# A first norm by row factors: centred weights, a factor per pixel from DRAM, and x turned three images ahead

## The chip, the cores and the metric

The kernel runs on one core of a Trainium2 chip. The metric is the device time of one execution in microseconds. A core has TensorE (matrix products and transposes into PSUM), VectorE, ScalarE and GpSimd (element work), SyncE (here it only issues transfers, on one queue) and 16 DMA engines. Each engine works off its own list in order, and engines wait for each other through semaphores.

## The reference

The input x has 16 images of 128 channels and 32 x 32 pixels. One block of a network is computed, in float32:

```python
# _ln_c: norm over the 128 channels of each pixel, eps 1e-6
x = x + conv(_ln_c(x))
#   conv: q, k, v = w_qkv @ net (8 heads of 32); k = softmax(k) over the 1024 pixels
#         context = k v^T per head; out = context q; w_out @ out + b_out
t = tokens(x)                       # (16, 1024, 128)
# _ln_t: norm over the 128 channels of each token, eps 1e-5
t = t + ffn(_ln_t(t))
#   ffn: feat = mean over the 16 images; w = softmax(feat @ Wr + br)  (1024 x 8)
#        8 experts: relu(bn(x W1 + b1)), relu(bn(. W2 + b2)), . Wo + bo; sum weighted by w
x = channels(t)
```

The weights of the experts belong to the pixel's place, and depend on the mean over all images. So the experts can't start before all images are through the attention and the second norm.

## The kernel before, in words

**First pass, in rounds.** `rounds` (L204) runs a `step` for t = -2 to 15; one round handles image t, prepares image t+1 and t+2, and finishes t-1 to t-3. On each engine the body of `step` is the list in its order. Per image:

- SyncE loads x (channels by pixels). TensorE turns it into tokens (`turn`, L539, into `p_k`), ScalarE copies it to `xT` (L778), VectorE takes `bn_stats` (L1039) and seven small operations (`statistics`, L1051), and GpSimd the power -1/2 and the shift (L1240, L1242). So each token has a factor RSTD and a SHIFT.
- GpSimd makes xn in token layout, `xnT` (`norm`, L1244, eight pieces of 128 x 128, L1248). TensorE turns xn back to channels (`turn_xn`, L504, into `p_tok`), ScalarE rounds it to `xn_hi` (L796), VectorE takes the rest, `xn_lo` (L996). All large products are sums of three: hi x hi, lo x hi, hi x lo.
- `k_half` (L548): k = wk xn, 2 x 6 products of 512 columns. VectorE finds each row's maximum (`head_max`, L1067), ScalarE takes the exponential E (`exp_half`, L840). TensorE turns E by halves (`turn_e`, L565, four times four transposes, all into one bank `p_e`), ScalarE copies it (`move_e`, L835), and `add_g` (L576) adds up G = xn^T E over the eight chunks, for each of two halves of the latent.
- In the next round: `gT` (L751), the product by heads (`heads_out`, L478), `y` (L967), `m` (L437), its high and low part (L766, L980), `add_m` (L487: M xn into `p_chan`), and x1 = x + M xn + b (L1011), stored to DRAM. So q, v, the context and w_out are folded into one 128 x 128 matrix M per image.
- In round t+2, x1 is turned and copied (`x1T`, L760), and has its statistics; its norm is shared by ScalarE (four pieces, L809) and GpSimd (four), into `xn2T`, and added to `feat` by GpSimd in round t+3 (L1300). The two rows SHIFT and RSTD are turned by one transpose (`turn_rows`, L496), copied (`move_rows`, L822) and stored to DRAM (L311), for the expert pass, which reads them back as rows over all partitions.

Weights are prepared in between: W1 and W2 are scaled by the batch norm, W1 is shifted by the mean (`shift_weights`, L521), w_out is spread by heads (L1020) and multiplied (L428).

**Passage.** Behind the last round the engines' lists are written out: the last x1, its norms, the mean `feat`, the logits, the routing (eight transposes of the routing into PSUM, copied to `routeT`, L913), 3 x 8 transposes that spread the weights of experts 0 to 2 over the partitions, the others by broadcast from DRAM (L350), with first products of experts in between.

**Second pass.** `slots` (L268): 16 images x 8 experts, three layers of 6 products each. TensorE is the one that never waits there.

The order around the change is fixed by hand: by the lists, by one SyncE queue for all transfers, and by the semaphores.

Of the kernel before, what the change touches and what calls it, by code (L numbers as in the profile page):

```python
# [24 lines left out]
F32 = mybir.dt.float32  # L25
# [20 lines left out]
TWO_MEAN, DIFFERENCE, SQUARES, BETWEEN, MINUS_MEAN, WITHIN, VARIANCE, SHIFT, RSTD = range(9)  # L46
# [13 lines left out]
def metaformer_kernel(nc, x, w_qkv, w_out, b_out, Wr, br, W1, W2, Wo, small, bo, ident_in, heads_in, out):  # L60
# [20 lines left out]
    MIDDLE = 6  # L81
    x1_dram = nc.dram_tensor("x1_scratch", [IMAGES, C, PIXELS], F32, kind="Internal").ap()
    rows_dram = nc.dram_tensor("rows_scratch", [IMAGES, 1, 2 * PIXELS], F32, kind="Internal").ap()
    route_dram = nc.dram_tensor("route_scratch", [EXPERTS, PIXELS], F32, kind="Internal").ap()

    with ExitStack() as ctx:  # L86
# [46 lines left out]
        const = sb("const", [128, len(CONSTANTS), CHUNKS])  # L133

        x_in = [route_all[:, p] for p in (6, 7)]
        x_res = [sb(f"x_res{p}", [C, PIXELS]) for p in range(2)]
        xnT = [as_tokens(n) for n in (4, 5)]
        sb("spacer", [128, 48])
# [3 lines left out]
        ekT = [as_tokens(n) for n in (2, 3)]  # L142
# [10 lines left out]
        rows_out = [sb(f"rows_out{p}", [2 * CHUNKS, 128]) for p in range(2)]  # L153
        row_bias = sb("row_bias", [2 * CHUNKS, 1])
        rows = sb("rows", [128, 2 * PIXELS])
        st = [sb(f"st{k}", [128, CHUNKS, 6]) for k in range(2)]
        ln = [sb(f"ln{k}", [128, 9, CHUNKS]) for k in range(2)]
# [4 lines left out]
        p_late = banks(6, 2)  # L162

        ident_loaded, small_loaded = sem("ident_loaded"), sem("small_loaded")
        x0_loaded, x0_turned, x0_copied = sem("x0_loaded"), sem("x0_turned"), sem("x0_copied")
        xn0_turned, xn0_hi_done, xn0_lo_done = sem("xn0_turned"), sem("xn0_hi_done"), sem("xn0_lo_done")
# [3 lines left out]
        in_loaded = [sem(f"in_loaded{p}") for p in range(2)]  # L170
# [6 lines left out]
        wT_done, wk_hi_done, wT_moved = sem("wT_done"), sem("wk_hi_done"), sem("wT_moved")  # L177
# [6 lines left out]
        xnt_done, x1t_done, last_turned = sem("xnt_done"), sem("x1t_done"), sem("last_turned")  # L184
# [8 lines left out]
        norm1_first = sem("norm1_first")  # L193
        stats_done = [stats1_done, stats2_done]
        sums_done = [sem(f"sums_done{k}") for k in range(2)]
        terms_done = [sem(f"terms_done{k}") for k in range(2)]
        var_done = [sem(f"var_done{k}") for k in range(2)]

        rstd_done = [sem(f"rstd_done{k}") for k in range(2)]
        ln_done = [sem(f"ln_done{k}") for k in range(2)]  # L200
        norm2_middle = sem("norm2_middle")
        norm1_done, norm2_last, feat_done = sem("norm1_done"), sem("norm2_last"), sem("feat_done")

        def rounds(engine, step):  # L204
# [4 lines left out]
            for t in range(-2, 5):  # L209
                step(t, t % 2, **valid(t))  # L210
# [3 lines left out]
            for t in range(IMAGES - 3, IMAGES):  # L214
                step(t, t % 2, **valid(t))
# [1180 lines left out]
```

## Time and profile before

| | us |
|---|---|
| three runs | 793.59, 792.53, 790.49; median 792.53 |
| the profiled execution | 792.24 |
| its span (first to last instruction) | 790.4 |
| start, up to the k product of image 0 | 15.05 |
| the 16 rounds, to the last G product | 223.2 |
| passage | 43.9 |
| expert stretch | 494.66 |

All intervals come from one profiled execution. An engine that is busy for a whole stretch sets its length. A busy share over the span averages over stretches with different limits, so the stretches are looked at one by one. The last four rows of the table are cut at the k product of image 0, at the end of the last product G (238.25), and at the last wait of TensorE ahead of the experts (282.11).

### The profile page before, as it was taken

Reading aid. Unit: us, or ns where it says so; the run is one execution under the profiler, and the core shown is the slowest. Engines: PE = TensorE matmul, PEld = TensorE weight load, DVE = VectorE, ACT = ScalarE, POOL = GpSimd, SP = SyncE. Lnnn points to the kernel's source line nnn. Section 1 sums busy time; section 2 is a strip of 40 time slices with the busy share of each in tenths; the row PEclk is TensorE's granted clock in tenths of the full one; section 3 lists DMA queues with packets and bytes.
Section 4 is the critical chain, followed back from the end, with each engine's and each line's share of the span. In section 5 each row is a group of like instructions: output and inputs, shape, how many; then the busy total and the mean of one; then the engine's idle time right before and its main releaser. Section 6 shows DMA issues by size and latency. Waiting matters only on the chain.

```text
span 790.4 us, 12762 instructions
## 1 busy us (share of the span) xinstructions
PE 775.7 (98%) x4242; PEld 648.6 (82%) x4242; DVE 527.0 (67%) x980; ACT 435.6 (55%) x570; POOL 650.9 (82%) x518
## 2 busy tenths in 40 slices
PE   8999999999998989999999999999999999999998
PEld 6998889889886778888888888888888888888886
DVE  5688787878787656666566665666656666566665
ACT  3576767676765655455454554545545455454543
POOL 5669888888888578888888888888888888888874
PEclk9999999999999999999999999999999999999999
DMA  8124233242531423031130311303113031130100
GB/s 249 54 81 142 101 124 117 99 142 80 214 120 44 158 110 134 0 134 67 67 133 0 133 60 73 133 0 133 62 71 133 0 133 59 74 133 1 54 27 27
DMA packets 22767, 72.58 MB, mean 92 GB/s; under 512 B 2880, under 2 KB 7624, under 8 KB 20688
## 3 DMA queue, kind: packets, MB, share of 16 engines
q1 hardware_dynamic: 22736, 72.19, 25.5%
q8 instruction: 17, 0.28, 0.2%
q14 instruction: 14, 0.11, 0.0%
HBM read 55.24 MB, written 16.94 MB: 91 GB/s over the span
## 4 chain that ended last, share of the span: by engine, by line
PE 67%; DVE 1%; POOL 1%; ACT 1%; issue 1%; POOLq 0%; DVEq 0%; ACTq 0%
PE psum L594 64%; PE psum L545 1%; PE psum L584 0%; PE psum L602 0%; POOLq L86 0%; POOL h_lo L1278 0%; ACT h_hi L853 0%; PE psum L702 0%; PE psum L717 0%; POOL xn2T L1248 0%; POOL ln L1240 0%; DVE st L1039 0%; DVE ln L1056 0%; PE psum L573 0%; DVE x_res L1127 0%
## 5 line engine op out<-in xcount | busy, mean ns | idle before, releaser
L1081 DVE SCALAR_TENSOR_TENSOR h_lo<-psum,h_hi 128x1024 fp32r<-128x1024 f32 x128 | 156.8, 1225 | 191.1 <-ACT h_hi L853 191.1
L853 ACT ACTIVATE h_hi<-psum 128x1024 fp32r<-128x1024 f32 x128 | 131.6, 1028 | 236.0 <-PE psum L594 236.0
L1278 POOL TENSOR_TENSOR h_lo<-w_raw,h_hi 128x1024 fp32r<-128x1024 f32 x64 | 154.1, 2409 | 41.8 <-ACT h_hi L872 41.8
L594 PE MATMUL psum<-h_hi,w_hi 128*128 128x512 f32 x382 | 118.5, 391 | 2.3 <-DVE w_raw L1102 2.3
L1102 DVE SCALAR_TENSOR_TENSOR w_raw<-psum,minus_t,route_all 128x1024 f32<-128x1024 f32 x93 | 118.6, 1275 | 1.7 <-DMA route_all<-route_scratch 1.1
L594 PE MATMUL psum<-h_lo,w_hi 128*128 128x512 f32 x382 | 119.4, 394 | 0.0
L594 PE MATMUL psum<-h_hi,w_lo 128*128 128x512 f32 x382 | 118.4, 391 | 0.0
L1278 POOL TENSOR_TENSOR xn_lo<-feat_most,xn_hi 128x1024 fp32r<-128x1024 f32 x31 | 74.7, 2409 | 36.0 <-ACT xn_hi L872 36.0
L594 PEld LDWEIGHTS psum<-h_hi,w_hi 128*128 128x128 f32 x382 | 71.4, 188 | 19.7 <-issue 2.7
L594 PEld LDWEIGHTS psum<-h_lo,w_hi 128*128 128x128 f32 x382 | 71.9, 188 | 15.6
L1240 POOL TENSOR_TENSOR ln<-ln,const 128x8 f32<-128x8 f32 x32 | 52.6, 1643 | 38.5 <-DVE ln L1065 38.5
L594 PEld LDWEIGHTS psum<-h_hi,w_lo 128*128 128x128 f32 x382 | 71.8, 188 | 15.2
L594 PE MATMUL psum<-xs_lo,w_hi 128*128 128x512 f32 x252 | 78.5, 393 | 0.0
L594 PE MATMUL psum<-xs_hi,w_hi 128*128 128x512 f32 x252 | 78.1, 391 | 0.0
L594 PE MATMUL psum<-xs_hi,w_lo 128*128 128x512 f32 x252 | 78.1, 391 | 0.0
L1278 POOL TENSOR_TENSOR xn_lo<-w_raw,xn_hi 128x1024 fp32r<-128x1024 f32 x32 | 77.0, 2405 | 0.9 <-ACT xn_hi L872 0.9
L872 ACT CAST h_hi<-w_raw 128x1024 fp32r<-128x1024 f32 x64 | 66.7, 1042 | 2.2 <-DVE w_raw L1102 2.2
L584 PE MATMUL psum<-route_all 128*128 128x128 f32 x512 | 65.7, 276 | 0.0
L584 PEld LDWEIGHTS psum<-route_all 128*128 128x128 f32 x512 | 62.8, 191 | 1.3
L845 ACT ACTIVATE route_all<-psum,negmax 128x1024 f32<-128x1024 f32 x32 | 35.7, 1116 | 36.8 <-DVE negmax L1074 36.0
L594 PEld LDWEIGHTS psum<-xs_hi,w_hi 128*128 128x128 f32 x252 | 47.1, 188 | 10.7
L594 PEld LDWEIGHTS psum<-xs_lo,w_hi 128*128 128x128 f32 x252 | 47.3, 188 | 10.2
(192 smaller groups left out, 1489.7 us busy)
## 6 DMA issues: line engine op xcount, KB each, us to landing
rows<-rows_scratch SPq DMA_DIRECT2D x16, 1024.0 KB, 7.3
x_res<-in_x SPq DMA_DIRECT2D x16, 512.0 KB, 3.4
x_scratch<-x_res SPq DMA_DIRECT2D x16, 512.0 KB, 2.8
xs_in<-x_scratch SPq DMA_DIRECT2D x16, 512.0 KB, 5.2
x_res<-x_scratch SPq DMA_DIRECT2D x16, 512.0 KB, 3.3
route_all<-in_x SPq DMA_DIRECT2D x15, 512.0 KB, 3.8
out<-x_res SPq DMA_DIRECT2D x15, 512.0 KB, 2.6
route_all<-route_scratch SPq DMA_DIRECT2D x5, 512.0 KB, 6.3
```

The lines of the kernel that those rows point to most:

```text
L545: mm = pe.transpose(dst[0:rows, 128 * n:128 * (n + 1)], chunk(n), ident[:])
L584: mm = pe.matmul(p_g[:, 128 * j:128 * (j + 1)], xnT[p][:, chunk, :], ekT[j][:, chunk, :], start=chunk == 0, stop=chunk == CHUNKS - 1)
L594: mm = pe.matmul(dst[:, px], w[:, which, e, :], part[:, px], start=first and w is w_hi and part is hi, stop=last and part is lo, skip_grou ...
L845: nc.scalar.activation(ek[j], k_out[j], ACT.Exp, bias=negmax[:, j:j + 1], accum_out=sums[p][:, j:j + 1]).then_inc(exp_done, 1)
L853: nc.scalar.activation(h1_hi[r][:], z1[r] if src is None else src, ACT.Relu).then_inc(h1_hi_done, 1)
L872: nc.scalar.copy(h2_hi[r][:], h2w[r]).then_inc(h2_hi_done, 1)
L1081: nc.vector.scalar_tensor_tensor(out=h1_lo[r][:], in0=z1[r] if src is None else src, scalar=0.0, in1=h1_hi[r][:].bitcast(F32), op0=ALU.max ...
L1102: nc.vector.scalar_tensor_tensor(out=h2w[k % RING], in0=z, scalar=minus_t2[:, e:e + 1], in1=weights, op0=ALU.max, op1=ALU.mult).then_inc(h ...
L1240: nc.gpsimd.tensor_tensor(o[:, RSTD], o[:, VARIANCE], const[:, MINUS_HALF], ALU.pow).then_inc(rstd_done[k], 1)
L1278: nc.gpsimd.tensor_tensor(h2_lo[r][:], h2w[r], h2_hi[r][:].bitcast(F32), ALU.subtract).then_inc(h2_lo_done, 1)
```

## The change

**No mean in the first norm.** The rows of `w_qkv` are centred (their mean over the 128 channels is subtracted, by VectorE: `centre`, three calls), so the mean of x drops out and SHIFT of the first norm isn't needed. What is left is a factor RSTD per pixel. `xnT` goes.

**The factor, twice.** In channel layout, the factor runs along the free axis: `turn_rows` now turns three rows (24 x 128: RSTD of x of image t+2, SHIFT and RSTD of x1 of image t-3), they go to DRAM, and SyncE reads RSTD back as a row over all 128 partitions (512 KB); GpSimd multiplies x by it in place (`scale_x`). For the product G, the tokens of x stay as they are and ScalarE multiplies the copy of turned E by RSTD (a factor per partition). For image 0 the factor is spread by eight transposes instead. TensorE's `turn_xn` goes.

**Three ahead.** x is turned in round t for image t+3 (before: t+2), into four token buffers, and four buffers hold x. The rounds -2 and -1 go: what they did is written ahead of the rounds, and partly moved into round 0 (the scales, the product by heads, the turning of images 2 and 3, Wo and W1's shift behind the turned E). The loop's body has four rounds (before: two).

**Turned E** is cut by pairs of chunks for both halves of the latent, and lies in `p_e`, twice in `p_tok`, and `p_e`; `add_g` has one product of 256 columns per chunk where it had two of 128.

**Statistics** of x (image t+2) and x1 (image t-3) are taken together, on 16 columns; x1's norm comes a round later than before and is GpSimd's alone up to image 10.

**Passage.** The routing is turned by one transpose (64 rows), goes to DRAM, and comes back as `routeT`; the fourth expert's broadcast goes first; ScalarE's order changes (`h1_high(6)` ahead of `h2_high(3)`).

```diff
 # TensorE
-            def turn_xn(t, q):
-                pe.wait_ge(norm1_done, t + 2)
-                pe.wait_ge(exp_done, 2 * t + 2)
-                turn(p_tok, lambda n: xnT[q][:, n, :]).then_inc(xnt_done, 1)
+            def step(t, r, s, n, a, c, f, d):
+                k_half(t, p, 0)
+                k_half(t, p, 1)
+                if at(t, 0):
+                    product_by_head(1)
+                    pe.wait_ge(wout_spread, 2)
...
+                    spread_scales(p_chan, S1)
+                    pe.wait_ge(by_head_moved, 1)
+                    turn_rows(-1, 3, p_e)
+                    turn_x(2, 2, 1)
...
+                if s and not at(t, 0):
+                    turn_x(t + 3, (r + 3) % 4, 2 * t + 1)
...
+                turn_e(t, 0)
+                turn_e(t, 1)
...
+                if c:
+                    pe.wait_ge(m_lo_done, t)
+                    wait(pe, copy2_done, t - 1)
+                    add_m(q)
+                turn_e(t, 2)
                 if at(t, 0):
+                    pe.wait_ge(expert_w, 6 * 16)
+                    shifts_through_wo()
+                add_g(t, r, 0)
+                turn_e(t, 3)
+                if at(t, 0):
+                    shift_weights()
+                    turn_x(3, 3, 1)
+                for i in range(1, 4):
+                    add_g(t, r, i)
+                turn_rows(t, r, p_e)
...
-                    mm = pe.matmul(p_g[:, 128 * j:128 * (j + 1)], xnT[p][:, chunk, :], ekT[j][:, chunk, :],
+                    mm = pe.matmul(p_g[:, 0:LATENT], x_tokens[r][:, chunk, :], ekT[:, chunk, :],
                                    start=chunk == 0, stop=chunk == CHUNKS - 1)
 # SyncE, in a round
+                store_rows(t, p)
+                if a:
+                    sp.wait_ge(rows_stored[p], stored_count(t, p))
+                    wait(sp, x_scaled, t)
...
+                    sp.dma_start(rstd_rows(t), rows_dram[t, 0:1, PIXELS:2 * PIXELS].to_broadcast([128, PIXELS])).then_inc(r_loaded, 16)
...
+                    sp.wait_ge(xn_lo_done, t + 1)
+                    sp.dma_start(x_in[r], x[t + 4]).then_inc(in_loaded[r], 16)
 # ScalarE, in a round: gT, rows, two exponentials, x1T, mT_hi, E 0, E 1, x, xn_hi, E 2, E 3
+            def high_part(t, k, q):
+                act.wait_ge(x_scaled, t + 1)
+                wait(act, mx_done, t)
+                nc.scalar.copy(xn_hi[q][:], x_in[k]).then_inc(xn_hi_done, 1)
...
+                for n in range(2):
+                    chunk = 2 * i + n
+                    ins = nc.scalar.activation(ekT[:, chunk, :], e_out[i][:, LATENT * n:LATENT * (n + 1)], ACT.Identity,
+                                               scale=norms[:, (r + 2) % 4, RSTD, 0, chunk:chunk + 1])
+                ins.then_inc(e_moved, 1)
 # VectorE, in a round: maxima, y, statistics, mT_lo, bn_stats of x1, x1, xn_lo, bn_stats of x
+                if a:
+                    dve.wait_ge(xn_hi_done, t + 2)
+                    nc.vector.tensor_tensor(xn_lo[q][:], x_in[(r + 1) % 4], xn_hi[q][:].bitcast(F32), ALU.subtract).then_inc(xn_lo_done, 1)
 # VectorE, ahead of the rounds
+            statistics(-2, OF_X)
+            dve.wait_ge(attn_w, 4 * 16)
+            centre(2, 2, 0).then_inc(wk_centred, 1)
...
+            centre(4, 2, 1).then_inc(w_centred, 1)
+            scale_first(0)
+            scale_first(1)
...
+            halves(0, x_tokens[1], 1)
+            statistics(-1, OF_X)
+            centre(0, 2, 2)
 # GpSimd, in a round
+                if at(t, IMAGES - 2):
+                    shift_xs(0, 0)
                 if a:
-                    norm(0, xnT[q], x1T if at(t, -1) else xT, range(norm1_split(t + 1), CHUNKS), norm1_done)
+                    scale_x(t, (r + 1) % 4)
+                if n or d:
+                    statistics(t, r, slice(0 if n else 1, 2 if d else 1))
+                if at(t, IMAGES - 2):
+                    split_low(0, 0)
...
+                if d:
+                    norm2(t - 3, r, x1_tokens[q], range(norm2_split(t - 3), CHUNKS))
+                    add_feature(t - 3)
+                if at(t, IMAGES - 3):
+                    scale_xs(0, 0)
+                if at(t, IMAGES - 1):
+                    statistics(IMAGES, 0, OF_X1)
+                    norm2(IMAGES - 3, 0, x1_tokens[1], range(norm2_split(IMAGES - 3), CHUNKS))
+
+            def scale_x(t, k):
+                pool.wait_ge(r_loaded, 16 * t + 16)
+                pool.wait_ge(tx_done, t + 2)
+                nc.gpsimd.tensor_tensor(x_in[k], x_in[k], rstd_rows(t), ALU.mult).then_inc(x_scaled, 1)
```

## Rows read from the trace of the kernel before

**Rows 1.** The page: busy us (share of the span) and instructions of TensorE and its loads.
```profile
PE 775.7 (98%) x4242; PEld 648.6 (82%) x4242; DVE 527.0 (67%) x980; ACT 435.6 (55%) x570; POOL 650.9 (82%) x518
```

**Rows 2.** Windows: from:to, length, busy us (instructions) by engine, granted clock, DMA share, GB/s.
```profile
15.05:31.33 16.28, 15.98 (x124) 14.25 (x125) 11.12 (x36) 8.21 (x13) 6.49 (x17) 1.00 0.39 147
...
58.03:86.58 28.55, 27.71 (x225) 24.44 (x224) 23.34 (x85) 20.34 (x38) 25.50 (x39) 1.00 0.33 112
86.58:195.80 109.22, 109.22 (x892) 97.77 (x890) 87.25 (x337) 77.37 (x145) 92.84 (x153) 1.00 0.33 116
...
209.37:224.27 14.90, 13.32 (x107) 11.36 (x105) 11.86 (x29) 8.86 (x16) 14.21 (x17) 1.00 0.20 72
224.27:238.25 13.98, 13.68 (x103) 11.73 (x104) 10.81 (x33) 8.82 (x17) 10.86 (x16) 1.00 0.48 190
...
282.11:776.77 494.66, 494.66 (x2161) 405.93 (x2162) 306.73 (x255) 249.28 (x253) 425.14 (x179) 1.00 0.20 72
```

**Rows 3.** Timeline of TensorE in round 10: start us, length us, engine, line, operation.
```profile
154.79 0.47 PE L561 MATMUL psum<-xn_hi,wkT_hi 128*128 128x512 f32 x1
...
161.24 1.09 PE L545 MATMUL psum<-ident,route_all 128*128 128x128 f32 x8
...
164.07 1.05 PE L584 MATMUL psum<-route_all 128*128 128x128 f32 x8
164.96 0.60 PE L573 MATMUL psum<-ident,route_all 128*128 128x128 f32 x4
```

**Rows 4.** Groups of instructions of the run: count, busy us, mean ns, idle before.
```profile
L1300 POOL TENSOR_TENSOR feat<-feat,xn2T 128x1024 f32<-128x1024 f32 x13 | 31.2, 2399 | 0.1
...
L1240 POOL TENSOR_TENSOR ln<-ln,const 128x8 f32<-128x8 f32 x32 | 52.6, 1643 | 38.5 <-DVE ln L1065 38.5
L1248 POOL TENSOR_SCALAR route_all<-xT,ln 128x128 f32<-128x128 f32 x120 | 52.0, 456 | 0.1
...
L1242 POOL TENSOR_TENSOR ln<-ln 128x8 f32<-128x8 f32 x32 | 6.5, 203 | 2.5
...
L838 ACT COPY route_all<-psum 128x512 f32<-128x512 f32 x64 | 37.4, 584 | 26.7 <-PE psum L573 26.7
...
L1039 DVE BATCH_NORM_STATS2 st<-xT 128x6 f32<-128x128 f32 x128 | 26.3, 278 | 3.0 <-ACT xT L778 3.0
```

**Rows 5.** Timeline of ScalarE and VectorE in round 10.
```profile
155.28 0.35 ACT L751 COPY gT<-psum 128x256 f32<-128x256 f32 x1
...
159.21 1.12 ACT L845 ACTIVATE route_all<-psum,negmax 128x1024 f32<-128x1024 f32 x1
...
162.21 0.29 DVE L980 TENSOR_TENSOR mT_lo<-psum,mT_hi 128x128 fp32r<-128x128 f32 x1 [2.32 <-ACT mT_hi L766]
```

**Rows 6.** DMA issues: count, KB each, us from issue to landing.
```profile
rows_scratch<-rows_out SPq DMA_DIRECT2D x16, 8.0 KB, 1.4
...
route_all<-route_scratch SPq DMA_DIRECT2D x1, 512.0 KB, 3.9
...
xs_in<-x_scratch SPq DMA_DIRECT2D x16, 512.0 KB, 5.2
x_res<-x_scratch SPq DMA_DIRECT2D x16, 512.0 KB, 3.3
```

**Rows 7.** Timeline about 67 us, and line L1056: shortest/median/longest in ns.
```profile
66.36 2.40 POOL L1300 TENSOR_TENSOR feat<-feat,xn2T 128x1024 f32<-128x1024 f32 x1
67.04 1.75 DVE L1056 TENSOR_TENSOR ln<-st 128x8 f32<-128x8 f32 x1
...
L1056 DVE TENSOR_TENSOR ln<-st x32: 156/171/1746, 8.3 to 249.7; 128x8 f32<-128x8 f32 x32
```

**Rows 8.** Timeline of round 0: ScalarE and TensorE.
```profile
22.01 1.11 ACT L845 ACTIVATE route_all<-psum,negmax 128x1024 f32<-128x1024 f32 x1 [3.08 <-DVE negmax L1074]
...
24.26 1.04 PE L545 MATMUL psum<-ident,route_all 128*128 128x128 f32 x8
```

**Rows 9.** Timeline of TensorE at the start of the expert stretch.
```profile
282.11 0.70 PE L594 MATMUL psum<-h_hi,w_hi 128*128 128x512 f32 x2 [2.26 <-DVE w_raw L1102]
```

More of the change, by code:

```diff
@@ L169, in metaformer_kernel @@
         expert_w = sem("expert_w")
-        in_loaded = [sem(f"in_loaded{p}") for p in range(2)]
+        in_loaded = [sem(f"in_loaded{r}") for r in range(4)]
         res_loaded = [sem(f"res_loaded{p}") for p in range(2)]
@@ L339, in _ @@
             rounds(sp, step)
-            for image in range(IMAGES - 3, IMAGES):
-                store_rows(image, image % 2)
-                if image == IMAGES - 3:
+            for index in range(IMAGES, IMAGES + 4):
+                store_rows(index, index % 2)
+                if index == IMAGES + 1:
                     sp.wait_ge(x1_done, IMAGES)
@@ L797, in step @@
[L797 to L802 removed]
+                move_e(t, r, 0)
+                move_e(t, r, 1)
+                if s and not at(t, 0):
+                    copy_x(t + 3, (r + 3) % 4)
                 if at(t, IMAGES - 2):
                     first_xs_high(0)
[L805 to L811 removed]
+                if at(t, IMAGES - 1):
+                    h1_high(0, 0, p_k)
+                    norm2_high(t - 3, q)
@@ L812, in step @@
+                if a and not at(t, 0):
+                    high_part(t, (r + 1) % 4, q)
+                move_e(t, r, 2)
+                move_e(t, r, 3)
                 if at(t, 0):
+                    copy_x(3, 3)
+                    high_part(t, (r + 1) % 4, q)
                     act.wait_ge(expert_w, 6 * 16)
@@ L1131, in _ @@
             halves(1, xT, IMAGES - 1)
-            statistics(1, IMAGES - 1, LN_T_EPS)
+            statistics(IMAGES + 2, OF_X1)
             h1_low(2, 2)
@@ L1329, in _ @@
             for image, tokens in ((IMAGES - 2, x1T), (IMAGES - 1, xT)):
-                statistics(1, image)
-                pool.wait_ge(ln_done[1], image + 1)
-                pool.wait_ge(feat_done, image)
-                norm(1, xn2T, tokens, range(MIDDLE if image == IMAGES - 1 else norm2_split(image), CHUNKS), norm2_last)
+                statistics(image + 3, (image + 3) % 4, OF_X1)
+                norm2(image, (image + 3) % 4, tokens, range(MIDDLE if image == IMAGES - 1 else norm2_split(image), CHUNKS))
                 if image == IMAGES - 2:
```

687 lines of the change are left out of this document (341 added, 346 removed).

## The prediction

> **What bounds the kernel now.** I read the page's busy line first: TensorE is busy for 98% of the span [rows 1]. Then a table of stretches, cut where each image's k product starts; a length between two rows is the gap between their ends [rows 2]. The first image starts at 15.05 us; its round takes 16.28. The rounds of images 1 and 2 take 26.70 together, 3 and 4 take 28.55, 5 to 12 take 109.22 (13.65 each), 13 takes 13.57, 14 takes 14.90, and 15 up to its last g product 13.98. The passage to the experts takes 43.86, and then comes the expert stretch of 494.66, in which TensorE never rests. The change touches nothing inside the expert stretch, so it keeps its length, and everything is decided in the 282 us ahead of it. In rounds 5 to 12 TensorE's row is full (109.22 of 109.22), so a round lasts as long as TensorE's own list, unless a wait replaces what goes. GpSimd has 92.84 of 109.22 there and ScalarE 77.37: little slack on the first, some on the second.
>
> **The parts, in a steady round.** I write times from the k product's start, 154.79 in the round shown.
>
> TensorE loses the turning of xn: eight transposes, 161.24 to 162.16, 0.92 us [rows 3]. The g product has half as many matmuls, each twice as wide. Eight instructions of 128 columns (four products of two passes) take 0.89 us [rows 3]; if time goes by columns the 256-wide form costs the same, and I take that. The turned rows and turned E keep their counts. TensorE's list becomes 13.69 - 0.92 = 12.77.
>
> ScalarE's copies of turned E become two activations with a factor per partition, four times a round. Today one copy of 512 columns takes 0.585 [rows 4]. A 256-column copy takes 0.355 [rows 5]; the factor adds about 0.1 (the exponential with its bias takes 1.12 for 1024 columns, against 2 x 0.585 less one start), so a pair takes about 0.75 to 0.8, and between 0.6 and 1.1 at the bounds. ScalarE loses its half of the second norm, so its total barely moves. Its order does: the copy of E that stood ahead of the copy of x1 and the rows' copy that stood ahead of mT_hi leave that place. mT_lo, which waits for mT_hi, ran from 7.42 to 7.71 [rows 5]; I get mT_hi 6.7, mT_lo 7.0, and m's product from 7.1. TensorE could be there at 6.8: a wait of 0.3. From there: m's product 1.5 (162.56 to 164.07), then 4.4 (164.07 to 168.48) for g and the last turned E [rows 3, 5], and 0.11 for the rows' transpose. The round can end at 13.05, not 12.77.
>
> The new chain: gT's copy ends at 0.85 today [rows 5], and about 0.1 earlier after; the rows' copy is behind it (1.0); its store is issued at 1.2 and lands 1.4 later [rows 6]; SP waits for that, then issues a broadcast of 512 KB. The nearest row is the first broadcast of the routing, also with transfers right behind it: 3.9 [rows 6]. Bounds: 3.3 (a load with little beside it) and 5.2 (a load with 1 MB behind it) [rows 6]. So the factor lands at about 6.7; GpSimd multiplies x by it, a two-input pass of 1024 like feat's, 2.40 [rows 4]: 9.15; ScalarE's high part, 1.0: 10.3; the third and fourth copies of E stand behind it: 11.05 and 11.8, where TensorE wants them at 11.2 and 12.1. It just fits. From about 4.0 us on, each us of the broadcast is a us of the round.
>
> GpSimd in a round: minus eight norm pieces of 0.45, plus four (all eight of the second norm are its own now), plus 2.4 for x. The two powers become one over 16 columns. 8 columns take 1.64, at the same engine on which ordinary passes of 8 columns take 0.2 [rows 4], so the power is paid by the column, I take it: 3.1 (bounds 1.65 and 3.3). Sum: 2.4 + 3.1 + 0.6 + 3.5 + 2.4 = 12.0 of 13, against 11.7 of 13.65.
>
> xn_lo took one input from PSUM; now both lie in SBUF. What that means the trace shows: a VectorE sum of 8 columns whose median is 0.17 took 1.75, and ended at 68.79, just as GpSimd's feat sum ended at 68.76 [rows 7]. In the new order xn_lo is ready (10.35) while GpSimd is in its power (9.2 to 12.3). If the power holds VectorE off, xn_lo ends at 13.4 and the next k product starts at 13.5; if not, at 13.05. I take the middle, 13.3, bounds 13.0 and 14.2 (with a broadcast of 5.1).
> The Trainium skill ("SBUF — State Buffer", "Who interferes with whom") states that a VectorE instruction with two SBUF inputs and a GpSimd instruction that reads SBUF exclude each other for the whole instruction. It speaks against this change, and by it the round is 13.5. For GpSimd's two-input sums the trace agrees (1.75 against 0.17); no run here shows it for the power.
>
> **The sum.** Start: today the second exponential of image 0 is issued at 22.01 [rows 8]. After, VectorE does x's statistics, two centrings, the scaling, the low parts, the statistics of image 1 (eight pieces of 0.28 in 1.64 [rows 4], plus 0.9) and a third centring of about 1.0 ahead of the first maximum, and I get 22.2: the same. But then TensorE's work differs. Today the shift of the weights (3.68, up to 24.26 [rows 8]) and the products through Wo (1.85) are done while it waits, and 7.1 are left to do. After, all of it is queued behind the turned E: 3 x 0.44 + 1.85 + 0.86 + 0.44 + 3.68 + 0.87 (x of image 3, a round earlier) + 2.6 + 0.11 = 11.7 from 23.5, a wait of 1.2 for bo_full (behind two new passes of VectorE), and 0.8 for copy, high and low part of image 1, which stand behind the last transposes. Image 1 starts at 37.2 in place of 31.33: +5.9 (bounds +3.5 and +7).
> Rounds 1 and 2: 13.8 (the scaling of W2 and the statistics are ahead of mT_lo) and 13.2, +0.3. Rounds 3 and 4: round 3 has 14.2 us of GpSimd's work, of which round 4 pays a part: 27.7, -0.85. Rounds 5 to 12: 8 x 13.3 = 106.4, -2.8. Round 13: 13.1, -0.5.
> Round 14: GpSimd ends the scaling of xs late (8.2), then its shift (10.6) and only then x (13.1); high part and both copies of E behind it bring the g product's end to 16.9, the round to 17.0, +2.1 (0.3 if the power costs 1.65).
> Round 15 and the passage: every x1 is normed one round later, so one image more (power, four pieces, feat: 6.6) is left for the last round, where GpSimd has 3.1 free today [rows 2]: some 3.5 late. VectorE's norm piece waits for it in front of y of image 15: 2.3 late. I take +3.0. Against this: the routing's broadcasts start some 1.7 earlier, and the seventh high part no longer queues behind the last of h2, which is where TensorE waits 2.26 [rows 9]: -2.0. Net +1.0.
> Sum: 5.9 + 0.3 - 0.85 - 2.8 - 0.5 + 2.1 + 1.0 = +5.1. The profiled execution took 792.24 (span 790.4, 1.84 around it), 0.29 under the median of 792.53: 797.3, for a median 797.5.
>
> **Rivals.** 0.5% (4.0 us, 788.6 to 796.5) is about what a measurement of this kernel can tell from no change.
> A, the forecast: the start's order and GpSimd's lag in the last rounds cost 11, the rounds give back 4, the new order of the passage 2. 797.5, own range 792 to 802. For it: all of the waits are written into the order. Chance 0.45.
> B, the power is paid by the instruction (1.65 for 16 columns). Then GpSimd has 1.5 to spare a round; xn_lo isn't held; rounds 13.05 (-2.0 more), no debt in round 4 (-1.3), round 14 -1.8, the end -0.5. 792. Against it: 1.64 against 0.20 for the same 8 columns. Chance 0.15.
> C, the other side: TensorE's list stays the bound. The list is 0.92 shorter in 14 rounds, and if mT_lo, x and the factor all come in time (the broadcast under 3.7, mT_lo by 6.8) the 14 rounds give up to 12.9; with 1 lost in waits and the start's 5.9, and the lag at the end covered by the first expert products, 786 to 788, say 787. It decides at the wait ahead of m's product: without it, this case. For it: TensorE's row is full today, and the cut is real. Chance 0.22.
> D, the chain through DRAM sets the round: a broadcast of 4.7 or more, with x's and the residual's loads behind it on the same rings. Rounds 13.9 and over: +0.6 on twelve rounds over A. 804. Chance 0.18.
>
> Chances: faster by over 0.5%: C without its edge, 0.19; within: B, A's lower part and C's edge, 0.32; slower: D and the rest of A, 0.49. The range reaches from C's value to D's: 786.5 to 804.
>
> **What would show it.** (1) First k product of image 1 at about 37, and transposes of E ahead of the weights' shift. (2) Period of rounds 5 to 12 at 13.0 to 13.5, m's product waiting about 0.3 for mT_lo. (3) GpSimd's power over 16 columns at 3.1. (4) xn_lo longer than 1.2, ending with a GpSimd instruction. (5) Broadcast landing in 3.9, x's scaling starting at 6.8. (6) Round 14 near 17. (7) No 2.26 wait ahead of the expert stretch. The prediction is wrong if image 1 starts before 34, if rounds fall under 12.9 or rise over 13.8, or if the passage isn't later than the rounds make it.

## The result, and the profile after

The changed kernel takes 804.68 us (median of 4 runs, 801.99 to 806.41), the kernel before 792.48 in the same session. The ratio is 1.0153, with a 95% interval of 1.0131 to 1.0175: 12 us slower, where 5 were forecast, and 0.7 outside the range. The profiled execution has a span of 804.6 us and took 806.41; it is the longest of the four, 1.7 above their median, so the differences read from it below come to more than the 12. The kernel before took 792.0 to 792.8 (medians) in every later session, so times of different sessions are laid side by side as they are.

In the page's busy line after, TensorE has 9 us less of work than in [rows 1], and is idle for 37.8 us, against 14.7:

```profile
PE 766.8 (95%) x3863; PEld 625.6 (78%) x3863; DVE 540.3 (67%) x907; ACT 435.2 (54%) x602; POOL 647.2 (80%) x414
```

The stretches after, cut where each image's k product starts, as in [rows 2] (from:to, length, busy us of PE, PEld, DVE, ACT, POOL, granted clock, DMA share, GB/s):

```profile
14.33:36.10 21.77, 18.20 (x121) 14.97 (x121) 12.95 (x45) 11.68 (x25) 6.20 (x5) 1.00 0.36 120
36.10:52.87 16.77, 14.37 (x87) 11.90 (x88) 12.87 (x36) 8.84 (x17) 6.33 (x3) 0.90 0.35 127
52.87:78.09 25.22, 25.22 (x177) 21.14 (x175) 20.66 (x70) 18.91 (x37) 13.40 (x7) 1.00 0.45 169
78.09:96.79 18.70, 15.21 (x89) 12.41 (x88) 14.47 (x36) 9.15 (x18) 17.81 (x24) 0.82 0.32 114
96.79:148.58 51.79, 51.33 (x351) 42.05 (x349) 42.87 (x140) 36.05 (x72) 42.44 (x45) 1.00 0.47 164
148.58:165.01 16.43, 14.34 (x89) 11.74 (x88) 13.30 (x36) 9.16 (x18) 15.32 (x21) 0.90 0.34 128
165.01:190.97 25.96, 25.81 (x177) 20.98 (x175) 21.31 (x70) 18.07 (x36) 20.23 (x20) 1.00 0.47 163
190.97:205.71 14.74, 12.70 (x90) 10.56 (x88) 13.34 (x36) 9.09 (x18) 13.78 (x17) 1.00 0.29 109
205.71:218.33 12.62, 12.13 (x82) 9.75 (x80) 8.75 (x27) 8.09 (x17) 11.05 (x13) 1.00 0.74 243
218.33:237.84 19.51, 13.57 (x81) 10.84 (x80) 14.93 (x27) 10.76 (x22) 18.64 (x18) 0.83 0.29 98
```

There are two kinds of rounds. Nine of them (2, 3, 5 to 8, 10, 11, 13) take 12.6 to 13.4 us, as long as TensorE's shortened list or little more. Five (1, 4, 9, 12, 14) take 14.7 to 19.5. Against the kernel before: image 1 starts 4.8 later (36.10 against 31.33), rounds 1 and 2 cost 2.7, rounds 3 and 4 2.8, rounds 5 to 12 give 0.3, round 13 gives 1.0, round 14 costs 4.6, and from image 15's k (237.84 and 224.27) to the end of the span it is 0.6. Together 14.2, the difference of the two spans.

What a long round looks like, in round 4 (timeline of GpSimd, VectorE and the product that waits: start, length, engine, line, operation; in brackets the idle time before it and its releaser):

```profile
82.98 0.18 DVE L1117 TENSOR_TENSOR terms<-st 128x16 f32<-128x16 f32 x1
...
83.14 2.45 POOL L1414 TENSOR_TENSOR feat<-feat,xn2T 128x1024 f32<-128x1024 f32 x1
83.17 0.18 DVE L1119 TENSOR_TENSOR terms<-st 128x16 f32<-128x16 f32 x1
83.39 2.24 DVE L1121 SCALAR_TENSOR_TENSOR terms<-terms 128x16 f32<-128x16 f32 x1
...
85.56 2.35 POOL L1353 TENSOR_TENSOR route_all<-route_all,w_raw 128x1024 f32<-128x1024 f32 x1
85.62 2.32 DVE L1124 SCALAR_TENSOR_TENSOR terms<-terms,eps 128x16 f32<-128x16 f32 x1
87.97 0.17 DVE L1127 TENSOR_TENSOR terms<-terms 128x16 f32<-128x16 f32 x1
88.07 0.28 DVE L1048 TENSOR_TENSOR mT_lo<-psum,mT_hi 128x128 fp32r<-128x128 f32 x1
...
88.41 0.79 PE L509 MATMUL psum<-xn_hi,mT_hi 128*128 128x512 f32 x1 [3.49 <-DVE mT_lo L1048]
```

VectorE's seven small sums of a round's statistics take 0.17 each. Two of them take 2.24 and 2.32 here: each ends with the GpSimd pass beside it (83.14 + 2.45 = 85.59, 85.56 + 2.35 = 87.91). Such a sum is called held below. Behind them stands the low part of m (`mT_lo`), and behind that TensorE's product, 3.49 late. It is what [rows 7] showed for one sum; the kernel before has three such sums in its rounds (1.75, 1.23 and 2.23), all behind the low part of m in VectorE's list. Now the holds reach TensorE in five rounds of fourteen; single sums of 0.68 to 0.87 in rounds 7, 8 and 11 cost it nothing. The whole run's group of the waiting product (count, busy us, mean ns, idle before and its releasers) holds 16.1 us of such waits:

```profile
L509 PE MATMUL psum<-xn_hi,mT_hi 128*128 128x512 f32 x32 | 15.5, 483 | 16.5 <-DVE mT_lo L1048 16.1 <-DVE mT_lo L1210 0.3
```

15.8 of them are in the five rounds, which together are 23.1 us over five of 12.61. The rest is a lower clock. In round 4 the granted clock is 0.93 up to the end of the wait and 0.68 behind it (two windows):

```profile
78.09:88.40 10.31, 6.83 (x58) 5.58 (x56) 9.00 (x19) 6.52 (x13) 9.74 (x13) 0.93 0.45 156
88.40:96.79 8.39, 8.38 (x31) 6.83 (x32) 5.47 (x18) 2.62 (x5) 8.07 (x12) 0.68 0.16 62
```

From m's product to the next image's k it takes 5.86 and 5.87 us at a clock of 1.00 (rounds 5 and 13). Behind the waits of rounds 1, 4, 9 and 14 it takes 7.47, 8.39, 7.51 and 7.34, at a mean clock of 0.77, 0.68, 0.77 and 0.78 (in round 4 it is 0.50 from 88.4 to 92.0, the lower of TensorE's two levels of 1.2 and 2.4 GHz); behind that of round 12 it takes 5.87 at 1.00. That is 7.2 us for the clock, and with the waits it makes up the 23.1.

### The profile page after: what moved, and what is told of

Same layout as the page of the kernel before. It is cut to its first block, busy times and chain, and to the rows that moved or that the text cites. A ratio compares the mean times of both kernels' runs of the same rounds, so it can differ in the third digit from the quotient of the medians.

```text
span 804.6 us, 11858 instructions
## 1 busy us (share of the span) xinstructions
PE 766.8 (95%) x3863; PEld 625.6 (78%) x3863; DVE 540.3 (67%) x907; ACT 435.2 (54%) x602; POOL 647.2 (80%) x414
## 4 chain that ended last, share of the span: by engine, by line
PE 76%; DVE 8%; issue 6%; POOL 6%; ACT 2%; DMA 1%; SPq 0%; POOLq 0%; DVEq 0%; ACTq 0%
PE psum L613 63%; PE psum L603 4%; PE psum L577 2%; POOL xn2T L1345 2%; POOL norms L1329 2%; PE psum L558 2%; DVE rawmax L1133 1%; PE psum L591 1%; DVE terms L1117 1%; PE psum L509 1%; DVE st L1096 1%; DMA route_all<-in_x 1%; DVE terms L1121 1%; DVE terms L1124 1%; POOL route_all L1353 1%
## 5 line engine op out<-in xcount | busy, mean ns | idle before, releaser
L613 PEld LDWEIGHTS psum<-h_lo,w_hi 128*128 128x128 f32 x382 | 71.8, 188 | 15.6
L1329 POOL TENSOR_TENSOR norms<-terms,const 128x16 f32<-128x16 f32 (+1 forms) x21 | 48.5, 2308 | 10.3 <-DVE terms L1127 10.3
L1133 DVE TENSOR_REDUCE rawmax<-psum 128x1 f32<-128x512 f32 x64 | 42.3, 685 | 20.7 <-PE psum L577 20.6
L613 PEld LDWEIGHTS psum<-xs_lo,w_hi 128*128 128x128 f32 x252 | 47.3, 188 | 10.3
L613 PEld LDWEIGHTS psum<-xs_hi,w_lo 128*128 128x128 f32 x252 | 47.3, 188 | 10.0
```

Of the source, the lines that this page charges most:

```text
L613: mm = pe.matmul(dst[:, px], w[:, which, e, :], part[:, px], start=first and w is w_hi and part is hi, stop=last and part is lo, skip_grou ...
L1133: nc.vector.tensor_reduce(rawmax[:, j, n:n + 1], k_out[j][:, BANK * n:BANK * (n + 1)], AX.X, ALU.max).then_inc(max_done, 1)
L1329: ins = nc.gpsimd.tensor_tensor(norms[:, k, RSTD, ks], terms[:, VARIANCE, ks], const[:, MINUS_HALF].rearrange("p (k n) -> p k n", k=2)[:, ...
```

## The experiments

Two theories besides the one to be tested (T: VectorE's statistics, ahead of the low part of m in its list, are held by GpSimd's two-input passes) stood from the start. G: GpSimd is simply late in these rounds. S: the route of the factor rows through DRAM ends them. Each kernel is the changed kernel with the edit shown; `...` stands for lines left out. Rounds are told by their number, positions in us from the k product's start.

### e1: the low part of m ahead of the statistics

```diff
+                if c:
+                    dve.wait_ge(m_hi_done, t)
+                    nc.vector.tensor_tensor(mT_lo[:], ...)
                 if n or d:
                     statistics(t, ...)
...
-                if c:
-                    dve.wait_ge(m_hi_done, t)
-                    nc.vector.tensor_tensor(mT_lo[:], ...)
```

> VectorE's low part of m is taken ahead of the statistics in its order; nothing else changes. Theory T (held statistics): in rounds 1, 4, 9, 12 and 14 of the changed kernel m's product started 8.9 to 12.2 us after the round's start, against 6.8 in the others, because VectorE's small sums stood ahead of the low part and each waited for a two-input pass of GpSimd. So m's product starts at 6.7 to 7.0 in all rounds, rounds 9 and 12 fall from 16.4 and 14.7 to about 13, round 1 from 16.8 to about 14.5, rounds 4 and 14 (where the statistics still end 10 to 12 us in and the residual sum and the next low part are behind them) to about 15 and 17.5: together -11, the time about 794. Rival G (GpSimd is simply late in these rounds, so that x's scaling, the power or the norms end them): these rounds stay within 0.5 us of what they are, the time within 802 to 807. Rival S (the route through DRAM ends them): the same as G, with the scaling of x waiting for its broadcast ahead of each long round's end.

Measured: 805.01 us, ratio 1.0162 (1.0143 to 1.0181). The product of m starts at 6.7 to 7.1 in every round, and rounds 1, 4 and 9 fall to 12.6, 14.6 and 13.9. But the statistics now begin at 6.6 to 6.9, where x's scaling meets them in all rounds but 3 and 7, and rounds 5 to 11 take 13.7 to 14.1. Round 6 (VectorE, GpSimd, and TensorE's transpose of the rows, which stands ahead of the next k product):

```profile
112.00 2.39 POOL L1353 TENSOR_TENSOR z_early<-z_early,w_raw 128x1024 f32<-128x1024 f32 x1 [0.46 <-DMA w_raw<-rows_scratch]
112.14 0.29 DVE L1039 TENSOR_TENSOR mT_lo<-psum,mT_hi 128x128 fp32r<-128x128 f32 x1 [1.62 <-ACT mT_hi L811]
112.35 2.08 DVE L1117 TENSOR_TENSOR terms<-st 128x16 f32<-128x16 f32 x1
...
115.38 2.91 POOL L1329 TENSOR_TENSOR norms<-terms,const 128x16 f32<-128x16 f32 x1 [0.99 <-DVE terms L1127]
...
117.87 1.21 DVE L1059 TENSOR_TENSOR xn_lo<-z_early,xn_hi 128x1024 fp32r<-128x1024 f32 x1
119.20 0.28 PE L520 MATMUL psum<-ident,norms 128*24 128x128 f32 x1 [0.71 <-POOL norms L1336]
```

My expected time (794) was a miss, the mechanism is clearer for it: the low part took its 0.29 beside the same pass that held the sum right behind it for 2.08 (the low part has one input in PSUM, the sum has both in SBUF). The hold wasn't removed but moved, to what stands behind the statistics, and from five rounds to nearly all. GpSimd's power needs the statistics and sits idle 0.99 for them; TensorE's transpose of the rows needs the power and waits 0.71 for it here, and 0.5 to 0.9 in rounds 4 to 6 and 8 to 11. xn_lo, behind the statistics too, ends 0.12 before that transpose, so it would allow hardly an earlier k.

### e3: GpSimd's two-input passes in one-input form

```diff
-                nc.gpsimd.tensor_tensor(x_in[k], x_in[k], rstd_rows(t), ALU.mult)
+                for n in range(5):
+                    ins = nc.gpsimd.tensor_scalar(x_in[k][:, 128 * n:128 * (n + 1)], ..., ALU.mult, ALU.add)
```

and the same for the features' sum. This kernel leaves out what the passes compute (x isn't multiplied by its factor, the features aren't summed), and keeps their place, their waits and nearly their length.

> GpSimd's feature sum and its scaling of x are replaced by five one-input passes of 128 columns with factors per partition each (0.448 each, so 2.24 and a pass of 0.2 ahead, against 2.39 for the pass replaced), at the same place in its order and behind the same waits; so x isn't scaled by the rows and the features aren't summed. Theory T: GpSimd is as busy and as late as before, but nothing holds VectorE: its statistics take 0.9 in every round but 14 (where two passes of the expert input, still with two inputs, run), rounds 1, 4, 9 and 12 fall to 14.4, 13, 12.9 and 12.9: about -12, the time 792 to 794. Rival G: GpSimd's load is what counts, and it is unchanged: 802 to 807. Rival S: the broadcasts are unchanged: 802 to 807.

Measured: 799.53 us, ratio 1.0086 (1.0066 to 1.0106). Rounds 1, 4, 9 and 12 take 13.65, 13.63, 12.85 and 12.63. GpSimd is busy as before (137.4 us in rounds 1 to 13, against 140.4), and its feature pass still begins amid the statistics (round 4):

```profile
80.30 0.19 DVE L1118 TENSOR_TENSOR terms<-st 128x16 f32<-128x16 f32 x1
...
80.75 2.22 POOL L1421 TENSOR_SCALAR feat<-xn2T,const 128x128 f32<-128x128 f32 x5
80.82 0.17 DVE L1124 TENSOR_SCALAR terms<-terms 128x16 f32<-128x16 f32 x1
...
81.10 0.17 DVE L1128 TENSOR_TENSOR terms<-terms 128x16 f32<-128x16 f32 x1
```

Rivals G and S are out for these rounds: the same load, the same broadcasts (4.2 us to landing, against 3.9), no round over 14 us but round 14, where two-input passes are left (18.9). Image 15's k came 13.5 us earlier (224.32), the run ended only 6.9 earlier. The missing 6.6 led to f1.

### e2: the features' sum a round later

```diff
+                if not isinstance(t, int) or t in (IMAGES - 4, IMAGES - 3):
+                    add_feature(t - 4)
                 if d:
                     norm2(t - 3, ...)
-                    add_feature(t - 3)
+                if isinstance(t, int) and t >= IMAGES - 3:
+                    add_feature(t - 3)
...
```

A tile of 32 bytes, which GpSimd clears once ahead of the rounds, is added for it, and the waits on the features' count go up by one.

> GpSimd's feature sum of image t-4 runs ahead of the norm of image t-3, a round later than before and straight behind the power (rounds 4 to 13), so that it no longer lies 3.2 to 5.6 us into the round, where VectorE takes its statistics; GpSimd's work is the same. Theory T: VectorE's first small sum takes 0.2 in place of 0.9 in rounds 6 to 12, the statistics end by 5.8, ahead of x's scaling (from 5.9 on), and rounds 4, 9 and 12 come to 12.7 to 13.2: -11, the time about 794; rounds 1 and 14, where the holder is x's scaling or the expert input's, stay at 16.8 and 19.5. Rival G: the same work on GpSimd gives the same lateness, long rounds remain (at the same or other numbers), the time 801 to 807. Rival S: as G.

Measured: 806.69 us, ratio 1.0191 (1.0172 to 1.021). Rounds 4 to 13 all took 12.6 to 13.3, and k of image 15 started 9.8 us earlier than in the changed kernel. But the rest of the run took 576.5 instead of 566.8, and all of the gain was lost. T had the rounds right, and neither theory had the loss.

### f1: a tile that nothing needs

```diff
         ln_wait = sb("ln_wait", [128, CHUNKS])
+        feat_tail = sb("feat_tail", [128, CHUNKS])
```

> The changed kernel with one unused tile of 32 bytes per partition added behind ln_wait, so that every later tile lies 32 bytes further on; no instruction differs. The two kernels with such tiles (one of 32 bytes, one with two of them) had their expert matmuls start every 232 ns (median gap) in place of 229. Theory P (place): the operands' addresses set this; the gap is 232 to 233 again, k of image 15 starts within 1 us of 237.8, and the stretch behind it is 576 in place of 566.8: the time 814. Rival: the slower pace came from the other order of the features' sum or from the chip's state; then the time is 803 to 807 and the gap 229.

Measured: 815.55 us, ratio 1.0308 (1.0281 to 1.0336), 10.9 over the changed kernel, with no instruction different. The same 480 us of the expert stretch, in the changed kernel and in f1 (TensorE full in both):

```profile
300.00:780.00 480.00, 480.00 (x2099) 393.84 (x2098) 297.90 (x248) 244.16 (x248) 415.44 (x175) 1.00 0.21 74
```

```profile
300.00:780.00 480.00, 480.00 (x2059) 386.12 (x2058) 291.43 (x243) 239.60 (x244) 406.65 (x171) 1.00 0.20 73
```

2059 matmuls in place of 2099, 1.9% fewer, at a granted clock of 1.00: with its tiles 32 bytes further on in a partition, the expert products follow each other more slowly (a mean of 233 ns from start to start against 229, a median of 232 against 229). e2 carried such a tile, and its stretch behind k of image 15 is that of f1 to 0.1 us (576.5): 9.7 of its time are this. e3 carried two, and its expert products start every 232 ns as well (median); that its 6.6 us are the same effect is likely, but its tiles weren't run alone. Which operand's place counts, and why, wasn't looked for.

f1 gives a second thing by accident: in its round 4 the wait is the same (m's product at 10.3), but the clock doesn't fall (two windows, to be laid beside those of the changed kernel above):

```profile
78.22:88.50 10.28, 6.83 (x58) 5.58 (x56) 8.98 (x19) 6.54 (x13) 9.76 (x12) 1.00 0.47 157
88.50:94.42 5.92, 5.86 (x32) 4.99 (x32) 5.53 (x19) 2.52 (x5) 5.63 (x6) 1.00 0.22 89
```

The round's rest takes 5.92 at full clock and 8.39 at 0.68: of round 4's 6.1 us of excess, 2.5 are the clock and 3.5 the wait.

### f2: e2 without its tile

The 32 bytes come out of an unused tile that the kernel has already (`spacer`); no operand moves.

> The features' sum a round later, as before, but with its 32 bytes taken out of the spacer, so that no operand moves. Theory P and T: rounds 4 to 13 take 130.6 as before (140.2 in the changed kernel), the stretch behind k of image 15 is 566.8 again, the time 795 to 797. If the slower pace belonged to the features' order, the time is 805 to 807 again.

Measured: 798.69 us, ratio 1.0096 (1.0075 to 1.0116), 6.0 below the changed kernel; the stretch behind k of image 15 is 566.8 again. Rounds 4 to 13, in the changed kernel and in f2:

```profile
78.09:218.33 140.24, 131.51 (x865) 107.48 (x863) 114.04 (x343) 89.61 (x179) 120.62 (x135) 0.96 0.44 154
```

```profile
77.64:206.94 129.30, 126.95 (x864) 104.61 (x863) 103.73 (x343) 89.38 (x179) 115.36 (x131) 1.00 0.48 167
```

The same instructions in another order on one engine (plus one of 8 columns ahead of the rounds), and ten rounds are 10.9 us shorter. VectorE's row loses 10.3 of its busy time, which was no work. I had expected 795 to 797: round 14 grew from 19.5 to 22.4. Round 1 fell from 16.77 to 15.13 with the same wait in it (2.38, against 2.40), since the clock stayed at 1.00 behind it; that is no gain of the edit.

### e4: the start's order

TensorE takes the products through Wo ahead of turned E of image 0; on VectorE the third centring moves from ahead of the first maximum to behind the shift of W1, and the bias sum to behind W1's scaling; ScalarE moves the second product by heads between its two exponentials.

```diff
                     turn_x(2, 2, 1)
+                    pe.wait_ge(expert_w, 6 * 16)
+                    shifts_through_wo()
...
-                if at(t, 0):
-                    pe.wait_ge(expert_w, 6 * 16)
-                    shifts_through_wo()
...
```

> Only the start's order differs: TensorE's products through Wo go ahead of turned E of image 0, ScalarE moves the second product by head between the two exponentials, VectorE takes the bias sum behind the scaling of W1, and the centring of the values' weights behind the shift of W1, so that the first maximum starts 1.07 earlier. If the start's loss lies in this order, TensorE's waits of 1.64 and 0.90 there go, and image 1 starts at 32.5 to 33.5 in place of 36.1: -3, the time 801 to 802. If it lies in x of image 1 (power, turned rows, store, broadcast, scaling, high and low part), image 1 starts no earlier than the chain allows, whose stores begin 0.9 to 1.2 earlier: 35, -1, the time 803 to 804. The long rounds behind it may move to other numbers; theory T leaves their causes where they are.

Measured: 799.78 us, ratio 1.01 (1.0067 to 1.0134). Image 1 starts at 34.16, after a round 0 of 19.56 in place of 21.77. That is 2.2 us for the round and 1.9 for image 1's start, between the two expectations: the order was part of it. TensorE's waits fall from 1.64 to 0.66 and from 0.90 to none, and it now waits 0.60 for xn_lo of image 1, as in the changed kernel. Most of the rest of the gain in time (round 9 at 12.7 in place of 16.4) is luck: x's scaling began at 6.5 there, not at 6.3, just behind the statistics.

### f3, f4, g1 to g3: orders together

Each of these carries several orders at once. f3 is f2, e4, the low part of m first in round 1 alone, and the residual sum of image 15 ahead of the statistics in the passage:

```diff
-            statistics(IMAGES + 1, OF_X1)
             dve.wait_ge(mx_done, IMAGES)
             nc.vector.scalar_tensor_tensor(out=x_res[1][:], ...).then_inc(x1_done, 1)
+            statistics(IMAGES + 1, OF_X1)
```

> f2 together with the start's order of e4, the low part of m ahead of the statistics in round 1 alone, and in the passage VectorE's residual sum of image 15 ahead of the last but one statistics (TensorE waited 2.86 for it, and the statistics were held 1.2 and 2.34 by the features' sum and the scaling of the expert input). Theory T: start -2 (image 1 at 34.2), round 1 from 16.8 to 13, rounds 4 to 13 -9.6, round 14 at 18 (the holder there, the expert input's two passes, is untouched), the passage -2.4: 786 to 788. Rival G (GpSimd's load): no more than the start's -2 and what f2 gives; 793 to 797.

Measured: 792.31 us, ratio 1.0001 (0.9987 to 1.0016). Round 1 takes 12.55 (16.77), rounds 4 to 13 129.6. Two misses: the passage gives nothing (567.7 from k of image 15 on, against 566.8), and round 14 is 22.30. In it GpSimd has four two-input passes in a row, and VectorE's small sums climb down them one at a time:

```profile
206.30 2.37 POOL L1419 TENSOR_TENSOR feat<-feat,xn2T 128x1024 f32<-128x1024 f32 x1
206.35 2.35 DVE L1119 TENSOR_TENSOR terms<-st 128x8 f32<-128x8 f32 x1
...
208.63 2.37 DVE L1120 TENSOR_TENSOR terms<-st 128x8 f32<-128x8 f32 x1
208.63 2.34 POOL L1361 TENSOR_TENSOR xs_in<-xs_in,rows 128x1024 f32<-128x1024 f32 x1
...
211.05 2.34 POOL L1366 TENSOR_TENSOR xs_in<-xs_in,rows 128x1024 f32<-128x1024 f32 x1
211.12 2.29 DVE L1123 SCALAR_TENSOR_TENSOR terms<-terms 128x8 f32<-128x8 f32 x1
...
213.34 2.35 POOL L1355 TENSOR_TENSOR z_early<-z_early,w_raw 128x1024 f32<-128x1024 f32 x1
213.40 2.31 DVE L1126 SCALAR_TENSOR_TENSOR terms<-terms,eps 128x8 f32<-128x8 f32 x1
```

f4 is f3 with the features' sum back where the change has it, and with another order of round 14, on GpSimd:

```diff
                 if a:
                     scale_x(t, (r + 1) % 4)
                 if n or d:
                     statistics(t, r, ...)
+                if at(t, IMAGES - 2):
+                    shift_xs(0, 0)
...
```

On VectorE the round's statistics stand behind the low part of m and the residual sum, ahead of xn_lo; the split of the expert input and its half layers go into round 15.

> As f3 but with the features' sum where the change has it, and with round 14 in another order: GpSimd scales x of image 15 ahead of the expert input's shift, VectorE takes the low part of m and the residual sum ahead of the statistics, and the split of the expert input and its two half layers go into round 15. Theory T: round 14 at 13 to 14 in place of 19.5, of which up to 3 come back in round 15 and the passage, since GpSimd has the same passes to do before the routing; rounds 9 and 12 may still meet the hold (each +2 to +4, by where the broadcast lands). 786 to 792. Rival G: round 14's excess moves whole into round 15 and the passage: 795 and more.

Measured: 793.88 us, ratio 1.0013 (0.9983 to 1.0044), above the 786 to 792 expected. Round 14 takes 13.70; 3.5 of the 5.8 us that this saves come back behind it (570.3 in place of 566.8). Rounds 4 and 12 are long again (17.6 and 14.7), as theory T has it for the features' sum in its old place.

g1 is f3 with this round 14, and the scaling of the expert input goes from ahead of x's to behind it and the power.

> f3 with round 14 in the order of f4, and the scaling of the expert input moved behind the scaling of x in that round, so that GpSimd goes features' sum (4.7 to 7.0 us into the round), x (to 9.4), power, expert input. Theory T: rounds 1 to 13 as in f3 (image 14's k near 201.7), round 14 at 13 to 14 in place of 22.3, and a stretch from k of image 15 on of 570 to 573 in place of 567.7, since GpSimd's passes for the expert input now lie in round 15: 786 to 789, 0.4 to 0.8% under the kernel before. Rival G: GpSimd has the same work ahead of the routing, so what round 14 gives back comes back whole behind it: 790 to 794.

Measured: 789.10 us, ratio to the kernel before 0.9959 (0.9945 to 0.9973): the first version here that beats both, the kernel before by 3.2 us and the changed kernel by 15.6. Its windows of round 1, of rounds 4 to 13 and of round 14:

```profile
34.28:46.83 12.55, 12.55 (x87) 10.58 (x88) 12.23 (x35) 8.65 (x17) 5.79 (x3) 1.00 0.49 169
72.22:202.93 130.71, 126.97 (x865) 104.57 (x863) 105.82 (x343) 89.50 (x179) 116.48 (x131) 1.00 0.47 165
202.93:216.35 13.42, 12.37 (x82) 9.68 (x80) 8.61 (x27) 8.93 (x20) 12.19 (x15) 1.00 0.37 136
```

g2 leaves the passage's change out:

> g1 without the passage's change (the residual sum of image 15 stays behind the statistics, which GpSimd's sums hold). Theory T as written for f3: +2 to +2.5 against g1. The other view, for which f3 speaks (its stretch behind k of image 15 was 567.7 against 566.8 without the change): another chain, GpSimd's norms of the last images, ends the passage, and g2 is within 1 us of g1.

789.32 us, ratio 0.9966 (0.9953 to 0.9978). So g2 beats the kernel before as well, and the passage is not ended by that residual sum, though TensorE waited 2.86 for it in the changed kernel. With the sum first (g1) that wait falls from 2.96 to 0.69, but the one for GpSimd's last features' sum, behind it, grows from 1.16 to 2.38: the transposes of that sum start 33.4 us after k of image 15 in both. g3 has the low part of m first in round 12 too:

```diff
-                if at(t, 1):
+                if at(t, 1) or at(t, 12):
```

> g1 with the low part of m ahead of the statistics in round 12 as well. In g1 round 12 took 14.4: no load of x runs there, the broadcast lands early and x's scaling starts 5.7 us into the round, while the statistics still run. Theory T: m's product starts at 6.8 in place of 8.5, round 12 takes 12.6 to 13.2, the time 787 to 788. Rival G: round 12 or 13 keeps the 1.7; 789.

792.08 us, ratio 0.9984 (0.9950 to 1.0018): a miss, since 787 to 788 were expected. Its times (790.48 to 792.89) lie above all of g1's (787.22 to 790.28), though the two ran in different sessions and the intervals of their ratios overlap. Round 12 falls from 14.4 to 13.2, since the hold moves on to the statistics as in e1, and GpSimd's power and features' sum start 0.8 and 1.5 later. That pushes the same collision into round 13, which grows from 12.6 to 14.75. The rounds from 1 to 14 are 1.3 us longer for it. With 0.4 at the start and 1.6 behind k of image 15, which the edit doesn't touch, the two spans differ by 3.4; so less than half of that is the edit's.

## Why the prediction was wrong

By its steps:

- **Where the rounds are decided.** "It decides at the wait ahead of m's product" (rival C) named the place. The forecast priced that wait at 0.3 a round; it is 0.3 or less in nine rounds and 2.0 to 5.7 in five. The failed step is this one: "mT_lo 7.0, and m's product from 7.1. TensorE could be there at 6.8: a wait of 0.3." It times mT_lo from mT_hi alone. The statistics, which the change puts ahead of mT_lo (in the kernel before they stood behind it), have no term in that step; only the sentence on rounds 1 and 2 names them there, and what could lengthen them is named nowhere. [rows 7] had shown such a sum held for 1.75, and that row was spent on xn_lo alone, which in fact runs beside the power. What a row says of one kind of instruction has to be carried to every instruction of that kind that the change puts near the cause, and here the change also added a second two-input pass to each of GpSimd's rounds.
- **xn_lo and the power.** "I take the middle, 13.3": refuted. In round 6 the low part ran inside the power at full speed:

```profile
105.34 2.92 POOL L1329 TENSOR_TENSOR norms<-terms,const 128x16 f32<-128x16 f32 x1
106.68 1.23 DVE L1059 TENSOR_TENSOR xn_lo<-z_early,xn_hi 128x1024 fp32r<-128x1024 f32 x1
```

- **The power's price** by the column: right, 2.91 on 16 columns (3.1 assumed); rival B's price is out, as 16 columns cost 1.77 times what 8 do (1.64). Its "xn_lo isn't held" came true, but not for its reason.
- **The steady round.** TensorE's list at 12.77: right, 12.6 to 12.9 in seven of the nine undisturbed rounds; from m's product to the next k it is 5.86, where the forecast's parts add up to 6.0. ScalarE's pair at 0.75 to 0.8: 0.83. The broadcast at 3.9: right, a median of 3.9 over the last 11, and rival D (4.7 and more in each round) is out; only round 7, where x's scaling begins at 7.2, shows what D meant, with 13.40. The load of x into x_res, issued behind it, now lands in 4.6 (median of 16).
- **Rounds 5 to 12** came to 108.9 in place of 106.4: six at about 13.0, and 9 and 12 with 5.2 us over that. Rounds 1 to 4, forecast at -0.55, cost 5.4: the same hold in round 1 (16.77) and twice in round 4 (18.70), two thirds of the miss.
- **Start:** +4.8 for 5.9, right in mechanism; e4 shows 2.2 of it to be the order written, and TensorE's wait for bo_full is there (0.90 for 1.2).
- **Round 14:** +4.6 for 2.1. The late scaling of x was seen, but not that VectorE's statistics would be held three times by the same passes.
- **From image 15's k on:** +0.6 for 1.0; TensorE's wait of 2.26 ahead of the expert stretch [rows 9] is 1.10 in its new place, and the expert stretch kept its pace.

The sum was 5.1; the spans differ by 14.2 (the medians by 12.2). Of the 9.1 between, 6.0 lie in rounds 1 to 4, 2.5 in rounds 5 to 12 and 2.5 in round 14, less the start's 1.1, the passage's 0.4 and the 0.4 of round 13. e3 and f2 show the hold to be the cause of rounds 4, 9 and 12, e3 and f3 of round 1, and f4 and g1 that the orders of GpSimd and VectorE set round 14. About 7 us of the 14.2 are the clock behind the waits, which no term of the forecast had; it follows only some of the waits, so another execution of the same kernel may pay less (the one of 801.99 had a mean clock of 0.991, the profiled one 0.987). Open is what decides this, and what ends the passage beyond GpSimd's last features' sum.

The measured 804.68 lies beside rival D's 804 (whose own terms, 797.5 + 12 x 0.6, give 804.7). That is luck: D's mechanism, a broadcast of 4.7 or more, did not occur in any of the 11 broadcasts of rounds 4 to 14 (3.3 to 4.5).

The Trainium skill ("SBUF — State Buffer", "Who interferes with whom") states that whoever issues first gets the pair of ports shared by VectorE and GpSimd for its whole instruction; that a VectorE instruction with two SBUF inputs contends for it with a GpSimd instruction that reads SBUF; and that a VectorE `tensor_scalar` can contend as well, in a two-port mode. The runs agree for GpSimd's two-input sums and scalings: VectorE's small sums that began with one took 2.0 to 2.4, while the low part of m, with one input in PSUM, kept its 0.29 beside one (e1). They agree in part for GpSimd's one-input pieces of 0.45: VectorE's small sums beside them took 0.16 to 0.39 in e3, and xn_lo, when it began first, made such a piece take 1.42 to 1.48 (rounds 4, 9 and 14 of the changed kernel). They differ for GpSimd's power, which has two SBUF inputs and held nothing. That the rule was applied to the power is what put the forecast's lost time into xn_lo.

## What to carry over

When one engine can hold another off, list for each critical instruction all that stands ahead of it in its queue, and ask of each whether it can be held and what runs beside it then; a 0.17 us instruction can cost 2.3. Moving the victim mostly moves the hold (e1, g3); moving the holder to where the other engine has nothing that it could hold removes it (f2). Ask too who waits for the victim: in e1 it was not the product that the edit had freed, but GpSimd's power and the transpose behind it. And keep every tile's address when an experiment adds one, or run the added tile alone.

## What the runs showed of the hardware that was not expected

- 32 bytes of displacement of the tiles slowed the expert matmuls by 1.9% (f1: 2059 against 2099 in 480 us) at an unchanged clock.
- GpSimd's power, with both inputs in SBUF, takes 2.92 us, and xn_lo inside it kept its 1.23; and a VectorE instruction with one input can be held: a `TENSOR_SCALAR` of 16 columns took 2.35 in round 12, from the start of x's scaling to its end.

```profile
196.91 2.35 POOL L1353 TENSOR_TENSOR route_all<-route_all,w_raw 128x1024 f32<-128x1024 f32 x1 [0.33 <-DMA w_raw<-rows_scratch]
196.95 2.35 DVE L1123 TENSOR_SCALAR terms<-terms 128x16 f32<-128x16 f32 x1
```

- It works both ways: in g1's round 12 VectorE's xn_lo started first, and GpSimd's features' sum took 3.37 in place of 2.4, about the overlap longer.

```profile
187.35 1.22 DVE L1063 TENSOR_TENSOR xn_lo<-route_all,xn_hi 128x1024 fp32r<-128x1024 f32 x1
187.42 3.37 POOL L1422 TENSOR_TENSOR feat<-feat,xn2T 128x1024 f32<-128x1024 f32 x1
```

- The same wait was followed by a fall of the granted clock in one execution and by none in another: 3.5 us in round 4 of the changed kernel (0.68 behind it) and of f1 (1.00), 2.4 us in round 1 of the changed kernel (0.77) and of f2 (1.00). Within the changed kernel, 2.09 us in round 9 were followed by 0.77, and 2.04 us in round 12 by 1.00.
